# A masked attention with routed experts: more masks copied into PSUM ahead of their product, and a gate product turned round

## The reference, cut to what matters

```python
def _L0_cond_ref(x, mask, conditioning, Wq, Wk, Wv, Wo, rms_scale, Wc, bc):   # H = 16, D = 16
    q, k, v = (proj(Wq), proj(Wk), proj(Wv))
    scores = jnp.einsum('bhsd,bhtd->bhst', q, k) * scale
    scores = jnp.where(mask[None, None, :, :], -jnp.inf, scores)
    attn = jax.nn.softmax(scores, axis=-1)
    out = jnp.einsum('bhst,bhtd->bhsd', attn, v)
    ...
def _L1_cond_ref(x, genre_embed, rms_w, wg_W, wg_b, gg_W, gg_b, W1, b1, W2, b2, W3, b3):   # TOP_K = 2, E = 8 experts
    xn = rms_w * (x * jax.lax.rsqrt(var + EPS))
    gate = xn @ wg_W + wg_b + (genre_embed @ gg_W + gg_b)
    gate_w = jax.nn.softmax(gate, axis=-1)
    topk_w, topk_i = jax.lax.top_k(gate_w, TOP_K)
    ...
x = x + _L0_cond_ref(...); x = x + _L1_cond_ref(...); x = x + _L2_cond_ref(...); x = x + _L3_cond_ref(...)
```

## Time and profile before

| what | value |
|---|---|
| runs | 1147.65, 1149.29, 1151.28 us (median 1149.29) |
| the profiled execution | 1151.16 us, of which the span of the trace is 1149.4 us |
| busy over the span | PE 97%, PE weight loads 68%, ACT 69%, DVE 66%, POOL 44% |
| mask products on PE (L1191) | 386 |
| mask copies by ACT (L1378) | 124 |
| gate products (L1244), 16 records in each of 8 batches | 128 |

### The profile page before, as it was taken

The page is one execution under the profiler, slowest core; times in us unless marked ns, Lnnn a source line. Parts: engine busy times, 40 slices in busy tenths (PEclk is TensorE's granted clock), DMA queues, the critical chain, the costliest instruction groups (busy, mean ns, idle before and its releaser), DMA issues.

```text
span 1149.4 us, 23356 instructions
## 1 busy us (share of the span) xinstructions
PE 1112.2 (97%) x7466; PEld 780.0 (68%) x7520; DVE 759.8 (66%) x2265; ACT 789.9 (69%) x1752; POOL 509.5 (44%) x837
## 2 busy tenths in 40 slices
PE   8899999999999999999899999989999999999988
PEld 4333434445344453444339999979999999999968
DVE  5887786787867878678744443455555555677547
ACT  2478787887878878788596567646666666666645
POOL 7413254756747567575643663552222222232220
PEclk9999999999999999999899999999999999999999
DMA  8663938558475583754747699664566666633536
GB/s 216 191 198 124 278 122 243 163 175 257 136 229 179 170 241 131 233 179 141 262 135 232 196 278 335 194 149 117 156 181 201 194 194 204 206 54 64 166 92 220
DMA packets 101617, 213.66 MB, mean 186 GB/s; under 512 B 10917, under 2 KB 71341, under 8 KB 93046
## 3 DMA queue, kind: packets, MB, share of 16 engines
q1 hardware_dynamic: 86038, 192.42, 52.6%
q0 software_dynamic: 14304, 18.69, 8.8%
q10 hardware_dynamic: 1152, 1.05, 0.4%
HBM read 239.28 MB, written 74.29 MB: 273 GB/s over the span
## 4 chain that ended last, share of the span: by engine, by line
PE 62%; DMA 5%; issue 4%; POOL 4%; DVE 3%; ACT 2%; another core or an unknown queue 0%; POOLq 0%; DVEq 0%; ACTq 0%
PE bank L1104 31%; PE bank L1206 6%; PE bank L1173 6%; PE bank L1187 5%; DMA x<-yout,rows 4%; PE bank L1191 3%; PE bank L1150 2%; PE bank L1159 1%; PE bank L1224 1%; PE bank L1119 1%; PE bank L1264 1%; POOL x L1993 1%; ACT pt L1372 1%; PE bank L1244 1%; DVE junk L1646 1%
## 5 line engine op out<-in xcount | busy, mean ns | idle before, releaser
L1646 DVE CUSTOM_DVE_ANT_0 junk<-bank,mneg 128x512 bf16<-128x512 f32 x512 | 332.3, 684 | 110.6 <-PE bank L1173 107.9
L1372 ACT ACTIVATE pt<-bank 128x512 f32<-128x512 f32 x512 | 294.2, 598 | 64.1 <-PE bank L1187 25.9
L1993 POOL DMA_INDIRECT x<-yout,rows x78 | 123.8, 1587 | 298.6 <-ACT yout L1456 252.1
L1104 PE MATMUL bank<-hid,w 128*128 128x256 f32 x1872 | 243.7, 287 | 4.7 <-DVE hid L1794 4.7
L1104 PEld LDWEIGHTS bank<-hid,w 128*128 128x128 f32 x1872 | 230.4, 191 | 6.7 <-issue 4.8
L1794 DVE TENSOR_TENSOR hid<-full,hid 128x256 fp32r<-128x256 f32 x312 | 134.2, 436 | 140.3 <-ACT full L1451 134.7
L1446 ACT ACTIVATE hid<-bank,biases 128x256 fp32r<-128x256 f32 x312 | 150.5, 482 | 96.1 <-PE bank L1104 88.7
L1451 ACT ACTIVATE full<-bank,biases 128x256 f32<-128x256 f32 x312 | 149.8, 480 | 0.5 <-DVE hid L1794 0.5
L1191 PE MATMUL bank<-mneg,identb 128*128 128x512 bf16 x332 | 127.2, 383 | 0.0
L1206 PE MATMUL bank<-pt,vaug 128*17 128x512 f32 x1024 | 123.3, 599 | 1.8
L1104 PE MATMUL bank<-w,hid 128*128 128x256 f32 x936 | 122.3, 284 | 2.7 <-DVE hid L1794 2.7
(11 more groups left out here) (184 smaller groups left out, 1459.9 us busy)
## 6 DMA issues: line engine op xcount, KB each, us to landing
w<-split_weights SPq DMA_DIRECT2D x80, 1024.0 KB
w<-split_weights SPq DMA_DIRECT2D x40, 2048.0 KB
split_weights<-w_parts SPq DMA_DIRECT2D x64, 512.0 KB
w_parts<-in_W SPq DMA_DIRECT2D x64, 256.0 KB
split_parts<-parts SPq DMA_DIRECT2D x28, 384.0 KB, 2.6
rows<-routed SPq DMA_DIRECT2D x39, 258.0 KB, 4.1
stacks<-split_parts SPq DMA_DIRECT2D x36, 256.0 KB, 6.8
qst<-split_parts SPq DMA_DIRECT2D x24, 256.0 KB, 6.3
```

The costliest lines, as they stand in the source:

```text
L1104: product = T.matmul(ps, w[p], x[q], start=(k == 0 and n == 0), stop=(k == len(weights) - 1 and n == 2))
L1372: A.activation(pt[n % len(pt)][:, :], ps[:, :], ACT.Exp, scale=float(D) ** -0.5).then_inc(exped.sem, 1)
L1646: V.tensor_tensor_reduce(junk[n % 2][:, :], ring_bank(step)[0][:, :], mneg[:, 0, st, :], 1.0, FLOOR, ALU.add, ALU.max, rowmax[gi % 2][:, h ...
L1993: G.indirect_dma_start(x2_dram, bass.IndirectOffsetOnAxis(ap=rows[j % NS][:, tt, E + 1:E + 2].bitcast(U32), axis=0), yout[j % NY][:, tt], ...
```

## The change

Two parts. **Masks:** in the key tiles with even `kt` ACT copies the mask of two heads, no longer of one. In the tiles with odd `kt` of groups with `gi % 4 < 2` (up to group 29) DVE copies a second one, right behind the row maximum three before the place (`ROWS_AHEAD`). The product L1191 goes for these. Over the program there are 186 copies by ACT instead of 124, 30 by DVE instead of none, and 294 mask products instead of 386. **Gate:** a zeroed `wg_wide` of 32 columns holds the scaled `wg` in its first 8 and becomes the stationary operand; x1T moves, 128 columns at a time. The four token tiles go to the four column groups, 8 products in all. ACT copies the 128 x 128 result to `gateT`, PE transposes that and adds the product of condR and ggw behind it, and ACT copies the logits as before. The chain of a batch gets one `yield` more, and one ring user more.

```diff
+GW = 32
+ROWS_AHEAD = 3
@@ chain
-    for _ in range(4):
+    for _ in range(2):
         yield
     out.append(("gate", b))
+    yield
+    out.append(("gate_copy", b))
+    yield
+    yield
+    out.append(("gate_turn", b))
     yield
     out.append(("logits", b))
@@ the plan of the copies
+    def early(user, at):
+        if user[0] == "row":
+            return row_place[user[1:]] <= rows_before[at] - ROWS_AHEAD
+        return user[0] == "col" and col_place[user[1:]] <= col_place[at] - ROWS_AHEAD
...
-            for hh in ((3, 2, 1, 0), (0, 1, 2, 3))[kt % 2]:
-                place = col_place[gi, kt, hh]
+            by_vector = kt % 2 and gi % NG < 2 and gi < GROUPS - 2
+            many = kt % 2 == 0
+            free = []
+            for hh in ((3, 1, 2, 0), (0, 2, 1, 3))[kt % 2]:
                 user = ring_before(("col", gi, kt, hh))
-                if user[0] == "row" or user[0] == "col" and col_place[user[1:]] <= place - SEED_AHEAD:
-                    seed_after[cols_at[place - SEED_AHEAD]] = gi, kt, hh
-                    break
+                if user[0] == "row" or user[0] == "col" and col_place[user[1:]] <= col_place[gi, kt, hh] - SEED_AHEAD:
+                    free.append((gi, kt, hh))
+            for at in free[:2 if many else 1]:
+                seed_after[cols_at[col_place[at] - SEED_AHEAD]] = at
+            for at in [at for at in free[1:] if by_vector and early(ring_before(("col", *at)), at)][:1]:
+                seed_behind[rows_at[rows_before[at] - ROWS_AHEAD]] = at
@@ gate, PE
-                for st in range(ST):
-                    for k in range(KT):
-                        T.matmul(ps[:, st * NX:(st + 1) * NX], x1T[:, k, st * P:(st + 1) * P], wg[:, k],
-                                 start=(k == 0), stop=(k == KT - 1))
+                for k in range(KT):
+                    for st in range(ST):
+                        product = T.matmul(ps[GW * st:GW * (st + 1), 0:P], wg_wide[:, k], x1T[:, k, st * P:(st + 1) * P],
+                                           start=(k == 0), stop=(k == KT - 1))
...
+                T.transpose(ps[:, 0:P], gateT[:, :], ident[:, :])
@@ gate_copy, ACT
+                A.activation(gateT[:, :], ps[:, 0:P], ACT.Copy).then_inc(gate_copied.sem, 1)
@@ row, DVE
+                after = seed_behind.get((gi, hh, st))
+                if after:
+                    ps, freed = ring_bank(("col", *after))
+                    dve.wait_ge(masks_made, MASKS)
+                    dve.wait_ge(*freed)
+                    V.tensor_copy(ps[:, :], mneg[:, 1, after[1], :]).then_inc(seeded_too.sem, 1)
```

More of the change, by code:

```diff
@@ L533, in _build @@
     wg = lasting("wg", [P, KT, NX])
+    wg_wide = lasting("wg_wide", [P, KT, GW])
+    gateT = lasting("gateT", [P, P])
     rmsw = lasting("rmsw", [P, KT])
@@ L641, in _build @@
     gated = signal("gated", of("gate"))
+    gate_turned = signal("gate_turned", of("gate_turn"))
     counted = signal("counted", of("place"))
@@ L657, in _build @@
     x1T_ready = signal("x1T_ready", of("turn_x1"))
-    logits_ready = signal("logits_ready", of("gate"))
+    gate_copied = signal("gate_copied", of("gate_copy"))
+    logits_ready = signal("logits_ready", of("gate_turn"))
     gate_exped = signal("gate_exped", of("gate_exp"))
@@ L765, in ring_before @@
         return ring_users[n] if n >= 0 else None
[L767 removed]
+    rows_before, n = {}, 0
+    for step in order:
+        n += step[0] == "row"
+        if step[0] == "col":
+            rows_before[step[1:]] = n
+    def early(user, at):
+        if user[0] == "row":
+            return row_place[user[1:]] <= rows_before[at] - ROWS_AHEAD
+        return user[0] == "col" and col_place[user[1:]] <= col_place[at] - ROWS_AHEAD
+    seed_after, seed_behind = {}, {}
     for gi in range(1, GROUPS):
         for kt in range(ST):
[L770 to L771 removed]
+            by_vector = kt % 2 and gi % NG < 2 and gi < GROUPS - 2
+            many = kt % 2 == 0
+            free = []
+            for hh in ((3, 1, 2, 0), (0, 2, 1, 3))[kt % 2]:
                 user = ring_before(("col", gi, kt, hh))
[L773 to L775 removed]
+                if user[0] == "row" or user[0] == "col" and col_place[user[1:]] <= col_place[gi, kt, hh] - SEED_AHEAD:
[4 more added lines that the diff above has]
+                seed_behind[rows_at[rows_before[at] - ROWS_AHEAD]] = at
     seeded = signal("seeded", [seed_after[at] for at in cols_at if at in seed_after])
+    seeded_too = signal("seeded_too", [seed_behind[at] for at in rows_at if at in seed_behind])
     project_place = {at: n for n, at in enumerate(projects)}
@@ L788, in evicted @@
         return {"project": rests, "project_v": v_ready, "modulation": gains, "maxima_rows": max_rows, "project_o": o_ready,
-                "turn_x1": x1T_ready, "gate": logits_ready, "place": ranks_ready, "mixed": mixed_ready, "turn": rows_split,
+                "turn_x1": x1T_ready, "gate": gate_copied, "gate_turn": logits_ready, "place": ranks_ready, "mixed": mixed_ready, "turn": rows_split,
                 "turn_x2": x2T_whole, "last": summed, "row": max_found, "col": exped}[name].at(at)
@@ L1239, in tensor_program @@
                 pe.wait_ge(prepared, PREPARED)
+                for k in range(KT):
+                    for st in range(ST):
+                        product = T.matmul(ps[GW * st:GW * (st + 1), 0:P], wg_wide[:, k], x1T[:, k, st * P:(st + 1) * P],
+                                           start=(k == 0), stop=(k == KT - 1))
+                product.then_inc(gated.sem, 1)
+            elif name == "gate_turn":
+                b, = at
+                ps = take(misc_bank(step))
+                pe.wait_ge(*gate_copied.at((b,)))
+                pe.wait_ge(ident_made, 2)
                 pe.wait_ge(dma_small, 16 * N_SMALL)
                 pe.wait_ge(constants_made, CONSTANTS)
-                for st in range(ST):
-                    for k in range(KT):
-                        T.matmul(ps[:, st * NX:(st + 1) * NX], x1T[:, k, st * P:(st + 1) * P], wg[:, k],
-                                 start=(k == 0), stop=(k == KT - 1))
-                T.matmul(ps[:, ST * NX:(ST + 1) * NX], condR[:, b:b + 1].to_broadcast([C + 2, P]), ggw[:, :],
-                         start=True, stop=True).then_inc(gated.sem, 1)
+                T.transpose(ps[:, 0:P], gateT[:, :], ident[:, :])
+                T.matmul(ps[:, P:P + NX], condR[:, b:b + 1].to_broadcast([C + 2, P]), ggw[:, :],
+                         start=True, stop=True).then_inc(gate_turned.sem, 1)
             elif name == "place":
@@ L1406, in scalar_program @@
                 b, = at
+                ps, _ = misc_bank(("gate_turn", b))
+                act.wait_ge(*gate_turned.at((b,)))
+                if b:
+                    act.wait_ge(*gate_pool.at(("logits", b - 1)))
+                A.activation(logits[:, :, :], ps[:, 0:(ST + 1) * GW].rearrange("p (s x) -> p s x", x=GW)[:, :, 0:NX],
+                             ACT.Copy).then_inc(logits_ready.sem, 1)
+            elif name == "gate_copy":
+                b, = at
                 ps, _ = misc_bank(("gate", b))
```

19 lines of the change are left out of this document (10 added, 9 removed).

## The result

The changed kernel takes 1158.61 us (median of 4 runs, 1156.44 to 1160.51), the kernel before beside it 1149.17 (4 runs). The ratio is 1.0087, 95% interval 1.0064 to 1.0110: slower, by about 9.4 us, where 18 us less were forecast.

The account below looks back on a forecast made before the run. PE's own work was taken to bound the attention stage up to about 553 us and nearly all the expert stage. -17.5 + 4.5 + 2.0 - 5.6 - 1.9 = -18.5 us gave a forecast of 1131 us, range 1124 to 1137.

Parts of the forecast that it names:

- the chain: Expert stage: one step more a batch puts the last batch's tables and pads eight blocks later; taken as zero, +-6.3 us possible.
- the second rival: Expert stage: the stretch round SP's eight stores moves, 1124.5 us with the whole gain, 1137 with the whole loss; chance 0.11.
- the charge of 4.5 us for waits: Attention stage, groups 1 to 27: 1.5 us for seven second iterations, 3.0 for DVE copies and four late places; bounds 0 to 11.8.
- the prediction's sign: Up to 550 us: PE's idle time ahead of column scores that names ACT's copy stays under 3 us in all.
- The end of the stage: End of the attention stage, ACT the bound: four more ACT copies in groups 30 and 31 cost +2.0 us.
- the masks' size as work of PE: Groups 1 to 27, PE the bound: 80 mask products fewer at 0.22 us, 17.5 us off.
- the gate's size: Gate on PE: 0.98 us instead of 1.92, a gain of 0.94; 5.6 us in the attention stage, 1.9 in the expert stage.
- the DVE copy's duration: DVE's mask copy into a bank: taken as 0.6 us, should last 0.5 to 0.7 us.
- The range: Whole kernel: 1124 to 1137 us, from the bounds of the waits (0 to 11.8) and the stretch (+-6.3 at half).
- the first (copies turn into waits): Attention stage: DVE and ACT give banks back later; all 11.8 us charged instead of 4.5, 1138.3 us; chance 0.21.
- The third (the clock falls): Mid attention stage: waits for copies halve PE's clock, at most 5.1 us a fall; six falls give 1162 us; chance 0.05.
- The gate's products on four column groups: Gate: forecast side by side; the rival has them one after another, 10.2 us more, 1141 us; chance 0.05.

Follow-up runs that it names:

- the fourth experiment: The kernel before with one yield more in each batch's chain and nothing else; 1155.50 us, 1.0064.
- the first: The kernel before with the masks' copies alone (186 by ACT, 30 by DVE), gate and chain of before; 1150.14 us, 1.0022.
- the third: The changed kernel with one yield less ahead of the gate, so the chain is as long as before; 1143.16 us, 0.9973.
- the seventh kernel: The third with `scale` two steps later in batches 0 to 4 and no new copies in the last four groups; 1131.78 us, 0.9868.
- the fifth: The third with `scale` to the counts two steps later in batches 0 to 4, chain length kept; 1135.05 us, 0.9894.
- tenth: The kernel before with `scale` two steps later and the place of tokens two steps sooner; 1145.59 us, 0.9990.
- ninth: The seventh kernel without the copies by DVE, their mask products back on PE; 1132.30 us, 0.9881.
- eighth: The third without the copies by DVE, their mask products back on PE; 1140.72 us, 0.9945.
- The twelfth kernel: The changed kernel, longer chain kept, with `scale` two steps later and the place two steps sooner; 1151.16 us, 1.0035.

## Why the prediction was wrong

The step that failed is the third of its parts, **the chain**. The prediction saw the `yield`, called its effect "the last batch's tables and pads eight blocks later", looked for that in the expert stage alone, and then wrote "I take zero". Taken out of the changed kernel it is worth 13 us, put into the kernel before it costs 7.4. Its price lies in the attention stage, where each batch's chain comes one pair later than the one before it had it. The expert stage, for which +-6.3 us were allowed, gained 3.6; between 742 and 772 us PE is busy for 29.20 us instead of 25.37, SP's eight stores have moved on to 762.38, and the fourth experiment, with the step alone, gained 5.8 there. But the first and the third, with the chain of before, gained 4.2 and 6.1 as well. So the stage did get shorter, within the bounds of the second rival, and that the moved `pads` are the cause is not shown.

The second step that failed is the charge of 4.5 us for waits, bounded by 11.8. It named the exponentials and row maxima that queue behind a copy, but all that it priced starts from a copy or from DVE's full first tile. In the seventh kernel, where little else is late, PE's waits for late copies came to about this size. Over the attention stage from batch 1 on PE waited there (us in total, times, longest):

```profile
PE bank L1217 <- ACT bank L1415: 4.5, 11, 1.3
...
PE bank L1217 <- DVE bank L1699: 0.5, 1, 0.5
```

What it left out is a wait that the trace of before has at 0.12 us a batch, unmarked: DVE's `scale` for POOL's root, at a distance counted in steps. Shorten the steps and the wait grows, in the third kernel to 1.0 to 1.8 us in each of five batches. Moving `scale` is worth 9 us of the third kernel's time, as the fifth shows. The fifth moves the steps up to the counts along with it, on the kernel before that is worth nothing (tenth), and no run moves `scale` alone. All late starts of PE in the five batches of the changed kernel sum to 19.6 us, above the upper bound; up to 550 us the idle time that names ACT's copy is 5.5 us, where the prediction's sign was under 3.

The end of the stage was sized too small: +2.0 us forecast, 4.2 measured by leaving the copies out. The prediction charged ACT's time for four copies; in the trace PE also waits for these copies every six us (0.75 to 1.18 us, the four rows above), and in the changed kernel once 2.25 us for DVE's.

Right were the masks' size as work of PE (batch 2 of the changed kernel, where PE is late by 0.5 us only, 68.70 us; five batches shorter by over 3 us without their late starts), the gate's size (0.93 us on PE for 0.98, 1.0 us a batch for 0.94) and the DVE copy's duration (0.69 us, in 0.5 to 0.7). As time, the 26 masks that DVE's copies replace brought nothing that can be told (ninth), though 5.7 of the 17.5 us are theirs. In the seventh kernel, with both steps mended and the end left alone, the sum's terms without the 2.0 for the end give 20.5 us; it has 15.2 by its ratio. The gap of 5.3 is about those 5.7, which fits and proves nothing.

The range does not follow from its own bounds: waits of 11.8 instead of 4.5 and half of 6.3 put its upper end at 1141 us, not 1137. The measured time is outside either.

Of the rivals, the first (copies turn into waits) had the right place, DVE's row maxima that come late, and half of the mechanism: DVE's own copies cost some 3 us (eighth), its wait for POOL more; its price was too small. The third (the clock falls) came true in part. Against it stood that the clock is full in all slices of the stage; a slice is 29 us long and does not show a short fall, and the kernel before has one, 3.4 us from 37.0 on. The changed kernel has one in the middle of the stage. PE there:

```profile
378.85 0.39 PE L1201 MATMUL bank<-kst,qst 96*128 96x512 bf16 x1 [1.44 <-DVE rest L1655]
...
380.08 0.39 PE L1217 MATMUL bank<-stacks 98*128 98x512 bf16 x1 [0.41 <-ACT bank L1415]
...
380.75 0.58 PE L1221 MATMUL bank<-mneg,identb 128*128 128x512 bf16 x1
381.12 0.63 PE L1201 MATMUL bank<-kst,qst 96*128 96x512 bf16 x1
381.54 0.63 PE L1217 MATMUL bank<-stacks 98*128 98x512 bf16 x1
```

and what DVE and ACT did ahead of it:

```profile
374.96 1.36 DVE L1747 SCALAR_TENSOR_TENSOR osb<-osb,ssq,gain_shift 128x256 f32<-128x256 f32 x1 [1.85 <-POOL ssq L893]
...
376.96 0.60 ACT L1415 ACTIVATE bank<-mneg 128x512 f32<-128x512 bf16 x1 [1.37 <-DVE rowmax L1692]
```

From 380.80 on the granted clock is at half, 1.2 GHz, for 3.4 us, and the score products follow each other at 0.43 us instead of 0.22. Six products start 0.21 late: 1.3 us in all. It comes behind the late `scale` and the two waits of PE. The Trainium skill (TensorE: Matmul & The Clock Gate, A second HAM failure mode: psum-queue depth-cycling) tells of a clock that goes down and up for short idle times between groups of products; this place agrees. Others do not: in the fourth kernel the clock stays full behind the wait of 3.20 us at 312.28, and falls for 3.4 us at 191.2, where PE has had no wait for 8 us. So that the late `scale` is the cause of this fall is not shown.

The changed kernel falls again at the end of the stage, at 578.8 for 6.8 us, right behind the wait of 2.25 us for a copy by DVE:

```profile
578.90 0.61 PE L1217 MATMUL bank<-qst,kst 98*128 98x512 bf16 x1 [2.25 <-DVE bank L1699]
...
583.36 3.00 PE L1236 MATMUL bank<-pt,vaug 128*17 128x512 f32 x16
```

A `weigh` of 1.91 us takes 3.00. The twelfth kernel has the same, a wait of 2.38 us and 6.8 us at half clock from 577.3 on; the third waits 0.48 us there, and its clock is full from there to the end of the stage. PE is busy for 6.38 of these 6.8 us, so the fall costs up to 3.2 us (an estimate), and the changed kernel takes 3.0 us longer than the third from the last row score to the last column score. So some 3 of the 13 us of the `yield` are probably this. The rival needed four falls of 5.1 us each; beside the fall that the kernel before has too (10.3 us long there, 6.9 here), there was one of 1.3 and one of about 3.

The gate's products on four column groups did run side by side. By their 0.67 us, four passes of 0.107 leave 0.24 for going into the form and out, as the 0.22 read from `weigh`. The Trainium skill (TensorEngine Tiling (Array Packing), Key Properties) states that a change of the tiling mode drains TensorE; the 0.24 us agrees with that.

## What to carry to other kernels

Where an order is written out in steps, a step more is not free because it carries no work: ask which work of other engines each later step now stands beside, for every round and not for the last. Before a bound engine is made faster, read for every cross-engine hand-over how long after the producer's end the consumer starts. Where it is as short as the hand-over itself (here 0.03 us), the consumer is waiting already, even if its idle time (0.12 us) is too short to be marked, and that wait grows with the change. And a lateness of that kind can be bought back by two steps' distance: it made some 9 us here, and nothing that can be told on the kernel before, whose batches are longer.

## What the runs showed of the hardware

DVE writes a PSUM bank from bf16 in 0.69 us (128x512, x30), the same as a product out of a bank, and above the 0.49 of a memset of a bank. The Trainium skill (VectorE: DVE Perf Modes, Why PSUM operands drop a tier) says that any PSUM operand caps an instruction at one of the 2x modes, and at 1x for fp32; the bank here is f32, and a time as long as the product's agrees.

An instruction of DVE that has waited for POOL starts 0.03 us behind POOL's end (310.23 and 310.26), and a column score that has waited for a mask copy 0.06 us behind the copy's end (median of the changed kernel's trace, the copies of ACT and of DVE alike).

`scale` itself takes from 0.44 to 1.36 us for the same shape in one trace of the changed kernel; the long ones shown above (302.70, 310.26) begin 0.08 us behind the start of a product of POOL on the parts (302.62, 310.18), and so does the one at 374.96 (374.88). Whether the one is the cause of the other no run tested.
